# One layer of attention and FFN in fp32 on one core: PSUM banks by kind of sum, pieces by key tile, later FFN transposes, and TensorE transposes at the end

## The reference

```
k, q, v = xn W_K[i], xn W_Q[i], xn W_V[i]        # 16 heads, 2048 x 128 each
scores = q k^T, causal mask, / sqrt(128)
attn = softmax(scores) ; z = attn v
attention = sum over heads of z W_O[:, i]
hidden = silu(xn W1^T) * (xn W3^T)               # 1024 wide
ffn = fwht(hidden) W2^T                          # Walsh-Hadamard transform, folded into W2
```

## Time and profile before

| | us |
|---|---|
| median of 3 runs | 1433.97 (1431.87 to 1434.05) |
| the profiled execution | 1434.14 |
| its span, first to last instruction | 1432.3 |
| mean granted TensorE clock | 0.983 of 2.4 GHz |
| TensorE (PE) busy | 1351.3 (94%), 8104 matmuls |
| DVE, ACT, POOL busy | 937.6, 947.6, 969.9 |
| hardware DMA queue | 334.65 MB, 74.4% of 16 engines |

### The profile page before, as it was taken

One profiled execution on the slowest core, in us unless ns is written; L12 is line 12 of the kernel. 1 busy time (PEld: TensorE's weight loads), 2 busy tenths in 40 slices (PEclk: granted clock), 3 DMA queues, 4 the chain that ended last, 5 costly groups with the idle time before them and its releaser, 6 DMA issues.

```text
span 1432.3 us, 26483 instructions
## 1 busy us (share of the span) xinstructions
PE 1351.3 (94%) x8104; PEld 1192.5 (83%) x8104; DVE 937.6 (65%) x2125; ACT 947.6 (66%) x1918; POOL 969.9 (68%) x640
## 2 busy tenths in 40 slices
PE   5999999889999999999999999999999999999985
PEld 4788888688888888888888888888888888888875
DVE  6533200577777777777777777777777777777760
ACT  4332244477877777878777777777777777777773
POOL 5130000077878787878797979797878787878785
PEclk9999999989999999999999999999999999999997
DMA  4200166588888889888888888898888888888784
GB/s 148 71 0 1 30 192 189 174 259 280 259 278 259 278 259 286 262 285 260 284 278 264 284 262 279 272 287 267 286 253 288 254 278 257 281 262 286 247 268 154
DMA packets 279263, 335.20 MB, mean 234 GB/s; under 512 B 62768, under 2 KB 251312, under 8 KB 274864
## 3 DMA queue, kind: packets, MB, share of 16 engines
q1 hardware_dynamic: 279216, 334.65, 74.4%
HBM read 173.08 MB, written 161.48 MB: 234 GB/s over the span
## 4 chain that ended last, share of the span: by engine, by line
POOL 38%; issue 23%; PE 22%; SPq 7%; DMA 5%; DVE 2%; ACT 2%; POOLq 1%; ACTq 0%; DVEq 0%
POOL pt_lo L401 26%; POOL acc L392 8%; PE ps L882 7%; PE ps L883 7%; PE ps L884 7%; SPq L297 6%; DMA scratch<-raw 4%; POOL v_lo L406 2%; ACT raw L587 1%; POOL wqk_lo L381 1%; DVE raw L824 1%; DMA pt_lo<-scratch 1%; POOL w_raw L359 1%; DVE had L814 1%; DMA acc<-x 1%
## 5 line engine op out<-in xcount | busy, mean ns | idle before, releaser
L401 POOL TENSOR_TENSOR pt_lo<-pt_lo,pt_hi 128x640 fp32r<-128x640 f32 (+11 forms) x384 | 661.6, 1753 | 144.3 <-ACT pt_hi L596 144.3
L587 ACT ACTIVATE raw<-ps,had 128x1024 f32<-128x1024 f32 (+7 forms) x384 | 329.0, 865 | 215.8 <-DVE had L817 201.9
L824 DVE STREAM_TRANSPOSE raw<-raw 128x2048 f32<-128x2048 f32 (+15 forms) x256 | 322.0, 1291 | 98.8 <-ACT raw L587 96.3
L882 PE MATMUL ps<-pt_hi,v_hi 128*128 128x256 f32 (+1 forms) x1152 | 328.4, 285 | 19.4 <-POOL pt_lo L401 13.2
L883 PE MATMUL ps<-pt_lo,v_hi 128*128 128x256 f32 (+1 forms) x1152 | 331.3, 288 | 0.0
L884 PE MATMUL ps<-pt_hi,v_lo 128*128 128x256 f32 (+1 forms) x1152 | 329.8, 286 | 0.0
L596 ACT CAST pt_hi<-pt_lo 128x640 fp32r<-128x640 f32 (+11 forms) x384 | 283.2, 818 | 19.2 <-DMA pt_lo<-scratch 19.2
L814 DVE TENSOR_REDUCE had<-ps 128x1 f32<-128x1024 f32 (+1 forms) x256 | 237.9, 949 | 59.6 <-PE ps L884 59.6
L882 PE MATMUL ps<-k_hi,q_hi 128*128 128x512 f32 (+3 forms) x640 | 239.5, 374 | 13.1 <-ACT raw L587 13.1
L882 PEld LDWEIGHTS ps<-pt_hi,v_hi 128*128 128x128 f32 x1152 | 222.3, 193 | 32.4 <-issue 18.7
L884 PE MATMUL ps<-k_hi,q_lo 128*128 128x512 f32 (+3 forms) x640 | 234.7, 367 | 0.0
(11 more groups left out here) (108 smaller groups left out, 2185.1 us busy)
## 6 DMA issues: line engine op xcount, KB each, us to landing
all_values<-raw SPq DMA_DIRECT2D x16, 1024.0 KB, 5.1
v_next<-all_values SPq DMA_DIRECT2D x16, 1024.0 KB, 5.5
scratch<-raw SPq DMA_DIRECT2D x64, 256.0 KB, 5.5
pt_lo<-scratch SPq DMA_DIRECT2D x16, 1024.0 KB, 5.3
scratch<-raw SPq DMA_DIRECT2D x64, 240.0 KB, 5.0
pt_lo<-scratch SPq DMA_DIRECT2D x16, 960.0 KB, 6.2
scratch<-raw SPq DMA_DIRECT2D x64, 224.0 KB, 5.4
pt_lo<-scratch SPq DMA_DIRECT2D x16, 896.0 KB, 4.7
```

The lines of the kernel that those rows point to most:

```text
L401: pool.tensor_tensor(lo, lo.bitcast(F32), hi.bitcast(F32), ALU.subtract).then_inc(pt_lo_done, 1)
L587: act.activation(to[:, first // P:(first + n) // P], ps[:, a * BANK:a * BANK + n].rearrange("p (i g k) -> p i g k", g=4, k=BLK), ACT.Exp, ...
L824: dve.transpose(v, v).then_inc(blocked, 1)
L882: pe.matmul(dst, a[0], b[0], start=start, stop=False, skip_group_check=True)
```

## The change

- **Banks.** Even sums and their outputs use bank 5 (BIG), odd ones bank 7 (SMALL), K and Q projections bank 6 (K0: bank 7; before head 0: banks 5 to 7 in turn). The ring is gone. A sum waits until the output two before it has been copied out by ACT.
- **Order.** On TensorE, the small sum comes before the output of the big one, and K2 at the end of step 7. On ACT, the odd z of steps 1, 3 and 5 is copied between the first and the second piece of that step, and K2 is copied behind the three pieces of step 7.
- **Pieces.** The two pieces of a big row are split by key tile (FIRST_KEYS), not by block of queries; a sum waits for its first piece and, at its first key tile of the second, for the second.
- **Start.** PAIRS_AFTER has the transposes of pairs 4, 5 after the fourth product and 6, 7 after the seventh, and before the Hadamard products; ACT does `had_copy(0)` and a weight copy before the silu table is loaded; the butterflies move.
- **End.** In the last head, the rows of steps 6 and 7 are neither transposed by DVE nor sent through DRAM: TensorE transposes them in 34 tiles of 128 x 128, in ten groups of up to four, and ACT and DVE split them from PSUM.

The diff, cut to its core:

```diff
+    FIRST_KEYS = {7: (8, 16), 6: (0, 7), 5: (0, 7), 4: (4, 10)}
     def key_order(c):
-        first = 8 if c in (4, 7) else 0
-        return list(range(first, 2 * c + 2)) + list(range(first))
+        a, b = FIRST_KEYS.get(c, (0, 2 * c + 2))
+        return list(range(a, b)) + list(range(b, 2 * c + 2)) + list(range(a))
+    def piece_keys(j, n):
+        a, b = FIRST_KEYS.get(j // 2, (0, j + 1))
+        b = min(b, j + 1)
+        return (a, b) if n != 1 else (b, j + 1) if a == 0 else (0, a)
...
-        RING_AT, Z = 5, 7
+        BIG, KQ, SMALL = 5, 6, 7
...
+        def z_bank(z, lo=0, hi=BANK):
+            return bank(SMALL if z % 2 else BIG, lo, hi)
+        def kq_bank(h, item):
+            if isinstance(h, int) and h < 0:
+                return bank(BIG + KQ_ITEMS.index(item) % 3)
+            return bank(SMALL if item == ("K", 0) else KQ)
+        def on_tensor(h, s):
+            return isinstance(h, int) and h == HEADS - 1 and s >= STEPS - 2
...
-        PAIRS_AFTER = {1: (2, 3), 2: (4, 5), 3: (6, 7)}
+        PAIRS_AFTER = {1: (2, 3), 3: (4, 5), 6: (6, 7)}
...
@@ ACT, start
+            had_copy(0)
+            gate_weights_to_hi(1, 0)
             act.activation(table_use[:, 1:2], ones[:, :], ACT.Silu)
...
@@ ACT, end of a step
                     hh, ss = step_before(h, s, 2)
-                        for n in range(3):
-                            p_to_hi(hh, ss, n)
+                    if over and s < 2:
+                        for n in range(5):
+                            transposed_to_hi(5 * s + n)
+                        p_to_hi(hh, ss, 0)
+                    if s in (1, 3, 5) and not absent(Z_SMALL[s][0]):
+                        z_to_hi(h + Z_SMALL[s][0], Z_SMALL[s][1])
+                        p_to_hi(hh, ss, 1)
+                        p_to_hi(hh, ss, 2)
+                    if s == 7 and more:
+                        kq_to_hi(h, ("K", 2))
...
@@ TensorE, start
                 gate_and_up(0, t)
+                for p in PAIRS_AFTER.get(t, ()):
+                    transpose_xn(p)
                 if t < 2:
                     had_products(t)
-                for p in PAIRS_AFTER.get(t, ()):
-                    transpose_xn(p)
...
@@ TensorE, project_kq
-                ring_wait(h, item)
+                if isinstance(h, int) and h < 0:
+                    wait(pe, proj_lo, kq_count(h, item) - 3)
+                elif item == ("K", 0):
+                    pe.wait_ge(shared, z_count(h, 1))
+                else:
+                    pe.wait_ge(proj_lo, kq_count(h, item) - (2 if item == ("K", 1) else 1))
...
@@ TensorE, weighted_sum
-                    wait(pe, z_lo_done, z_count(h, z) - 1)
-                    pe.wait_ge(pt_lo_done, piece_count(h, 2 * (z // 2) + 1, 2 if z % 2 else 1))
+                    wait(pe, shared, z_count(h, z) - 2)
+                    if behind_k:
+                        pe.wait_ge(proj_lo, kq_count(h, ("K", 0)))
+                    if on_tensor(h, 2 * (z // 2)):
+                        pe.wait_ge(t_lo_done, len(T_GROUPS) if z % 2 else 8)
+                    else:
+                        pe.wait_ge(pt_lo_done, piece_count(h, 2 * (z // 2) + 1, 2 if z % 2 else 0))
+                second = 0 if part is None else FIRST_KEYS[c][1] - FIRST_KEYS[c][0]
...
+                    if n and n == second and not on_tensor(h, 2 * (z // 2)):
+                        pe.wait_ge(pt_lo_done, piece_count(h, 2 * (z // 2) + 1, 1))
...
@@ TensorE, last period
+            def transpose_group(n):
+                s, small, a, b = T_GROUPS[n]
+                if n < 5:
+                    pe.wait_ge(exped, piece_count(HEADS - 1, STEPS - 1, exp_of(STEPS - 1, n)))
+                else:
+                    pe.wait_ge(t_lo_done, n - 4)
+                for i in range(a, b):
+                    ins = pe.transpose(bank(n % 5, (i - a) * P, (i - a + 1) * P),
+                                       raw_row(s, small)[:, i * P:(i + 1) * P], ident)
+                ins.then_inc(transposed, 1)
...
@@ TensorE, end of a step
                     if s == 7 and more:
                         project_kq(h, ("K", 1))
-                        project_kq(h, ("K", 2))
+                    if s in Z_SMALL and not absent(Z_SMALL[s][0]):
+                        weighted_sum(h + Z_SMALL[s][0], Z_SMALL[s][1], None, behind_k=s == 7 and more)
                     if s in O_BIG and not absent(O_BIG[s][0]):
                         output(h + O_BIG[s][0], O_BIG[s][1])
-                    if s in Z_SMALL and not absent(Z_SMALL[s][0]):
-                        weighted_sum(h + Z_SMALL[s][0], Z_SMALL[s][1], None)
+                    if s == 7 and more:
+                        project_kq(h, ("K", 2))
```

More of the change, by code:

```diff
@@ L424, in period @@
                     hh, ss = step_before(h, s, 2)
-                    if not (first and s < 2) and not (over and s >= 2):
+                    if not (first and s < 2) and not over:
                         for n in range(3):
@@ L536, in kq_to_hi @@
                 act.wait_ge(projected, kq_count(h, item))
[L537 removed]
+                act.activation(to, kq_bank(h, item), ACT.Copy, scale=1.0 if which == "K" else SCALE
                                ).then_inc(proj_hi, 1)
@@ L859, in period @@
                         kq_to_lo(h, ("K", 1))
-                    if not over:
+                    if not over and not on_tensor(h, s):
                         transpose_blocks(h, s, 1)
```

123 lines of the change are left out of this document (56 added, 67 removed).

## The result

The changed kernel takes **1418.63 us**, the median of 4 runs (1411.12 to 1419.54), against 1433.06 (1431.87 to 1434.05) for the kernel before in the same session. The ratio is 0.9888, with a 95% interval of 0.9853 to 0.9923: faster by 11 to 21 us. The forecast was 1385 with a range of 1371 to 1406. The sign was right, the size was not, and the range misses it by 13 us. The profiled execution took 1419.54, the longest of the four; its span is 1417.5.

A forecast was written before the change was run, and what follows sets the result against it. The prediction took TensorE to bound the kernel, busy nearly throughout, with DMA next (0.87 busy in head 7). Gains of 27.3 + 3.5 + 0.4 + 6 + 4.8 + 7 = 49.0 us from 1433.97 gave 1385, range 1371 to 1406.

The forecast's parts named there:

- Fourteen heads: 965.3, less 27.3: Heads 1 to 14: 68.95 us each, 965.3 in all against 992.6 before, a gain of 27.3 us.
- I add 0.25 a head for this: Step 3: ACT waits 1.7 us for row 1's landing, z7 and step 4's maxima slip 0.2; priced at 0.25 a head.
- hangs on the exponentials of step 4: Second part of sum 0: the v_lo stall of 0.82 us stays, as it depends on step 4's exponentials.
- Landings take it back: Rival for the heads: late DMA landings leave a win of 0.5 a head instead of 1.95, 1405 us; chance 0.19.
- Slower: K2 behind late pieces: Rival: row 5 lands late, K2's copy stops the next head's scores; 4.8 us a head, 1457; decides from 3.2; chance 0.05.
- More is won: Rival: v_lo comes on time (14 x 0.8) and the end wins 10, 1371 us; chance 0.07.
- It doesn't do what it says: Rival: sums stay coupled by single z buffers, late transposes only move waits to DVE; within 3 us of 1434; chance 0.02.
- Start: Before head 0: first down projection at 46.8 instead of 53.10, 6.3 earlier, less 0.3 for half-clock matmuls: 6 us won.
- Head 0: Head 0: 2.2 of sum 0's 3.63 wait, 0.3 at output 2, about 1 of half clock: 3.5 us won.
- Head 15: Last head, steps 0 to 6: 56 us expected instead of 60.8, a gain of 4.8.
- The end: From the last scores to the end: 35.8 us against 44.5, less 1.7 for a half-clock stretch: 7 won.
- The transposes hold the clock down: Rival for the end: transposes count as idle, sums and outputs run partly at 1.2 GHz, 7 to 8 us, 1393; chance 0.05.

The follow-up runs named there:

- run 15: The changed kernel with all bytes kept and each row stored by one DMA instead of four: 1414.32 us, ratio 0.9873.
- run 6: The changed kernel with SP's order in a step made load big, store big, load small, store small: 1402.55 us, ratio 0.9804.
- values ahead: The changed kernel with V's last two blocks in step 4 copied ahead of ACT's exponentials and split ahead of POOL's adds: 1415.56 us, ratio 0.9905.
- K2 first: The changed kernel with K2 projected before output 2 and copied on ACT ahead of the pieces of step 7: 1414.95 us, ratio 0.9887.
- run 2: The changed kernel with rows' stores and loads cut to half their bytes, same number of DMAs: 1380.02 us, ratio 0.9644.
- (14): The changed kernel with half of each row's bytes and three 1 KB transfers added ahead of each row's stores: 1550.53 us, ratio 1.0823.
- (11): The kernel before the change with SP's order made load big, store big, load small, store small: 1433.61 us, ratio 0.998.

## Why the prediction was wrong, and where it was right

**The step that failed** is "Fourteen heads: 965.3, less 27.3", and in it the term "I add 0.25 a head for this" for the landings at step 3. Heads took 71.0 on average, and the landings and what hangs on them cost 2.4 a head instead of 0.25. The wait itself was foreseen: ACT was to wait 1.7 us for row 1, and it waits 0 to 2.6, 1.3 on average. What was wrong is what the wait costs. I gave it the 2.4 us of room before sum 0 needs its piece. That room was there, no sum waits for pt_lo; but on POOL the adds and v_lo stand behind the same pieces, and on that path there was none. That v_lo "hangs on the exponentials of step 4" is so where the landing is in time: in head 11 ACT comes from these to the copy of output 7 at 1079.58 without idle time. POOL's first add, which that copy also waits for, ends at about 1079.5 (an estimate: half of the two adds' 2.53 us after 1078.22). The two paths are within 0.1 us of each other, so every later landing goes straight to v_lo (18.9 us of waits on TensorE for 17.9 on ACT). And a stall of 2.3 us can bring a half-clock stretch that costs 1.4 more, which I priced in head 0 and at the end, not here: 8.4 us in six heads. The rest is k_lo, 4.7, in heads 1 and 2 above all.

Two readings led there. Head 7 of the kernel before, with a landing at 8.3 where ACT gets there at 8.7, was taken for a head like the others; in seven of fourteen heads ACT already waited 0.4 to 1.7 for it. And I counted on loads issued up to 2.4 us sooner; row 1's load, which waits for its own stores and for no sum, was issued 3.1 us after scores(3) begin on average before and 4.0 after. Its store, the landing, the load, the copy and POOL's pieces don't shorten when PE does.

DMA stood in the text as "next", with no price. The trace of before had the engines busy for 61.0 us in a head of 70.9, and this doesn't shrink with the head: at 68.95 us it is 0.885. That was a reason to ask what the landings cost, but no price either: run 15 at 0.80 loses 1.9 us a head against 68.6, the changed kernel at 0.86 loses 2.4, run 6 at 0.91 loses 1.3.

**Rivals.** "Landings take it back" was the right mechanism with the wrong size: it let a head win 0.5, and heads won -0.07 (1.0 us over fourteen). "Slower: K2 behind late pieces" is there in heads 1 and 2 (2.17 us idle at 330.84 in head 1), far from the 3.2 a head at which it decides. (The worst wait of ACT for row 1 in the kernel before was 1.74, in head 13, and not the 1.66 of head 2 that the text weighs against it.) "More is won" didn't come: v_lo grew. "It doesn't do what it says" didn't either: the waits did move, and the time is below 1434 beyond the noise.

**Terms that held.** The bounds and the order of the work did what was said: the stalls of the exponential, output 6 and output 2 are gone, and so is that of sum 0 (but in head 14, where row 1 lands last, output 6 still waits 0.60); K2 costs 0.19 where nothing is late, forecast 0.2 to 0.3. A head without late landings takes 68.6, forecast 68.7. v_lo, forecast at 0.82, is 1.19 there (1.03 + 0.16).

**Start.** The first down projection came at 47.14, forecast 46.8, 5.96 earlier than the earlier trace rows. Then 1.0 of it was lost: the trace shows the clock at 0.50 from 47.8 for 3.4 us, where before it had been at full speed. I had taken off 0.3, and counted 0.4 won by the three banks, which is in this balance.

```profile
47.14 0.36 PE L930 MATMUL ps<-pt_hi,k_hi 128*128 128x256 f32 x1 [2.24 <-DVE pt_lo L784]
...
48.62 0.41 PE L930 MATMUL ps<-pt_hi,k_hi 128*128 128x256 f32 x1
48.83 0.41 PE L931 MATMUL ps<-pt_lo,k_hi 128*128 128x256 f32 x1
```

**Head 0** won 2.3 instead of 3.5. Its terms came: sum 0 waits 1.32, as 3.63 less 2.2 had it, and the time at half clock went from 17.0 to 6.8 us. What the sum didn't have are new stalls: 0.97 for q_lo, 0.98 for v_lo, 0.38 for z_lo and 0.99 that the trace puts down to no one. PE also waits 4.48 for an exponential where it waited 2.89, which fits its getting there sooner at full clock.

**Head 15** won 0.1 instead of 4.8. I let output 6's wait go, as in the other heads, but its row 1 landed at 11.7 us after scores(3), and it waits as before, with 6.8 us at half clock behind it (1.99 in the earlier trace rows):

```profile
1357.71 0.39 PE L930 MATMUL ps<-wo_hi,z_hi 128*128 128x256 f32 x1 [2.03 <-DVE z_lo L866]
1359.24 0.58 PE L930 MATMUL ps<-pt_hi,v_hi 128*128 128x256 f32 x1 [0.56 <-ACT aux L644]
```

**The end** was right, and one term of it too careful: the transposes began 6.5 us after the last scores, as forecast, and the last output 30.3 us after them, forecast 30.0. The 1.7 for half-clock matmuls didn't come.

```profile
1387.85 2.02 PE L1062 MATMUL ps<-identity,raw 128*128 128x128 f32 x17
...
1390.98 0.39 PE L930 MATMUL ps<-wo_hi,z_hi 128*128 128x256 f32 x1 [1.11 <-DVE z_lo L866]
...
1394.35 1.20 PE L1062 MATMUL ps<-identity,raw 128*128 128x128 f32 x9
1395.71 1.12 PE L1062 MATMUL ps<-identity,raw 128*128 128x128 f32 x8 [0.16 <-DVE pt_lo L873]
...
1411.70 0.39 PE L930 MATMUL ps<-wo_hi,z_hi 128*128 128x256 f32 x1 [0.97 <-DVE z_lo L866]
```

The window from 1387 to 1396 holds both groups of transposes and two stalls, and the granted clock is 1.00. So the rival "The transposes hold the clock down" didn't come about. The Trainium skill ("TensorE: Matmul & The Clock Gate", Part 4: PE-mode transpose) says that a transpose doesn't count as a busy engine for the clock in the same way; in this trace, with matmuls around groups of 17, nothing shows it. A longer run of transposes alone wasn't tried.

## What to carry to other kernels

When an engine is to be made faster, follow each transfer that is just in time to everything that stands behind it, on every engine in between, and not only to its nearest use: a wait of 1.3 us on ACT had 2.4 us of room on one path and none on another, and there it cost the full time. The busy time per period of what doesn't shrink (here 61 us of DMA in a head) over the new period is a reason to look, but not a measure: heads were nearly as late at a share of 0.80 as at 0.86, and less late at 0.91. To find out what landings cost, halve the bytes and keep the instructions, in the old kernel and the new one: by the ratios that gave 0.8% in the old one and 2.4% in the new one here, and the difference, 24 us, is what the landings took back. Removing the wait that shows the lateness didn't remove it (values ahead, K2 first and the pieces each moved it); what gained was fewer bytes, or another order of SP's loads and stores, and most with values ahead and K2 first on top of that order.

## What the runs showed of the hardware that was not expected

- A stall of the same length has two prices. In eleven heads of the changed kernel v_lo is waited for over 2.2 us; behind five of these the clock is granted at 0.50 for 3.4 us (heads 3, 6, 7, 8, 10), behind six at 1.00 (heads 1, 2, 5, 12, 13, 14). Head 12 and head 10 both have 2.31 in the trace.
- The issue of a row's store takes SP 0.45 us with half of the bytes and 0.72 on average with all, 15 of the 64 of a head over 0.9 us. One plain store of a whole row takes 0.46 with all bytes (15), and a load's issue 0.54 with half and 0.45 with all, so bytes alone don't set it; no run shows what does.
- Transfers of 32 elements of 4 bytes, under 0.1 MB in all, doubled the busy time of the engines (83.2 us a head against 40.2 in run 2) and the landing of V's load (10.4 against 5.3 us), and made the kernel 1.6 times as long. With one piece of 1 KB in their place (14) the engines are busy for 43.2 us and the same load lands after 5.1; that kernel is 1.08 times as long as the one before, with SP issuing for 68 of the 79 us of a head, 0.6 us for each such piece.
- Loading and storing in turn (6) raised the busy time of the DMA engines for the same 19.3 MB a head from 61.3 to 63.7 us, and the kernel was faster; in the kernel before (11) it went from 61.0 to 63.7.
